# Splitting weight chunks 3 to 13 with two DMAs and a negation instead of a load, a rounding and a subtraction

## The reference

```python
q, k, v = x @ wq.T, x @ wk.T, x @ wv.T          # heads of 128
q, k = rope(q), rope(k)
o = lightning_attention(q, k, v)                # scores * exp(-lam * (i - j)), causal
x = x + o @ wo.T
h = layernorm(x)
x = x + fwht(silu(h @ W1.T) * (h @ W3.T)) @ W2.T
```

## Time and profile before

| | before |
|---|---|
| median of 3 runs | 270.7 us (270.65 to 270.79) |
| profiled execution, its span | 269.5 us |
| PE busy | 261.0 us, 97% |
| DVE busy | 204.9 us, 76% |
| ACT busy | 167.7 us, 62% |
| POOL busy | 143.9 us, 53% |
| granted clock of PE | 1.00 all through |
| read from HBM | 11.93 MB |

### The profile page before, as it was taken

How to read it: one execution, slowest core, us unless ns; L and a number is a source line. 1 busy time by engine, 2 the same in 40 slices (tenths; PEclk the granted TensorE clock), 3 DMA queues, 4 the chain that set the end, 5 groups by cost and what they waited for, 6 DMA issues and landing times.

```text
span 269.5 us, 4222 instructions
## 1 busy us (share of the span) xinstructions
PE 261.0 (97%) x1506; PEld 227.4 (84%) x1506; DVE 204.9 (76%) x336; ACT 167.7 (62%) x283; POOL 143.9 (53%) x105
## 2 busy tenths in 40 slices
PE   7898799999999999999999999999999999999995
PEld 5786488979889888888889889898888879988895
DVE  4799899899979897869899799795575984143333
ACT  3879896875898767556867768984353542043230
POOL 2302989888889467532795897899519200000000
DMA  6594620211220000000020001200000000100002
GB/s 205 189 346 169 243 80 2 78 31 47 80 78 4 0 1 0 4 0 0 2 61 17 2 11 67 80 2 2 0 0 2 0 0 21 59 0 2 0 0 78
DMA packets 5635, 13.23 MB, mean 49 GB/s; under 512 B 624, under 2 KB 2544, under 8 KB 5616
## 3 DMA queue, kind: packets, MB, share of 16 engines
q1 hardware_dynamic: 5040, 12.39, 13.4%
q10 hardware_dynamic: 576, 0.59, 0.6%
HBM read 11.93 MB, written 1.05 MB: 48 GB/s over the span
## 4 chain that ended last, share of the span: by engine, by line
PE 72%; DVE 15%; ACT 5%; issue 4%; DMA 2%; POOL 1%; SPq 0%; DVEq 0%; ACTq 0%
PE bank L317 24%; PE bank L318 24%; PE bank L319 23%; DVE rope_b L1014 2%; DVE rope_a L1013 2%; DMA w_raw<-in_wq 2%; DVE bank L1041 2%; DVE v_hid L1000 1%; PE bank L333 1%; ACT rope_b L661 1%; ACT rope_b L660 1%; DVE qk L1021 1%; DVE rope_b L1065 1%; DVE o_lo L1051 1%; DVE p_lo L1046 1%
## 5 line engine op out<-in xcount | busy, mean ns | idle before, releaser
L843 POOL TENSOR_TENSOR qk<-rope_a,rope_b 128x512 f32<-128x512 f32 x36 | 49.7, 1383 | 25.6 <-DVE rope_b L1014 25.1
L317 PE MATMUL bank<-xt_hi,w_hi 128*128 128x512 f32 x140 | 55.0, 393 | 0.5 <-issue 0.4
L318 PE MATMUL bank<-xt_lo,w_hi 128*128 128x512 f32 x140 | 54.7, 391 | 0.0
L319 PE MATMUL bank<-xt_hi,w_lo 128*128 128x512 f32 x140 | 54.5, 389 | 0.0
L850 POOL TENSOR_TENSOR q_hid<-qk,q_hid 128x512 fp32r<-128x512 f32 x29 | 39.8, 1379 | 10.4 <-ACT q_hid L666 10.4
L673 ACT ACTIVATE p_hi<-bank 128x512 fp32r<-128x512 f32 x48 | 28.6, 596 | 15.7 <-DVE bank L1041 15.2
L1014 DVE TENSOR_TENSOR rope_b<-rope_b,sin_sb 128x512 f32<-128x512 f32 x40 | 37.7, 942 | 0.0
L318 PE MATMUL bank<-w_lo,o_hi 128*128 128x256 f32 x128 | 36.2, 283 | 0.0
L319 PE MATMUL bank<-w_hi,o_lo 128*128 128x256 f32 x128 | 36.2, 283 | 0.0
L317 PE MATMUL bank<-w_hi,o_hi 128*128 128x256 f32 x128 | 36.1, 282 | 0.0
L1013 DVE TENSOR_TENSOR rope_a<-bank,cos_sb 128x512 f32<-128x512 f32 x40 | 27.5, 687 | 10.6 <-ACT rope_b L661 10.1
(11 more groups left out here) (90 smaller groups left out, 614.8 us busy)
## 6 DMA issues: line engine op xcount, KB each, us to landing
w_raw<-in_w SPq DMA_DIRECT2D x6, 512.0 KB, 3.2
decay_sb<-in_decay SPq DMA_DIRECT2D x4, 512.0 KB, 5.3
w_raw<-in_wo SPq DMA_DIRECT2D x4, 512.0 KB, 4.7
w_raw<-in_wq SPq DMA_DIRECT2D x3, 512.0 KB, 3.3
x_sb<-in_x SPq DMA_DIRECT2D x3, 256.0 KB, 7.1
out<-x_sb SPq DMA_DIRECT2D x6, 128.0 KB, 1.8
w_raw<-in_wv SPq DMA_DIRECT2D x1, 512.0 KB, 6.1
w_raw<-in_wk SPq DMA_DIRECT2D x1, 384.0 KB, 6.4
```

The costliest lines, as they stand in the source:

```text
L317: pe.matmul(o, a_hi, b_hi, start=first, stop=False, skip_group_check=shared)
L318: pe.matmul(o, a_hi, b_lo, start=False, stop=False, skip_group_check=shared)
L319: return pe.matmul(o, a_lo, b_hi, start=False, stop=last, skip_group_check=shared)
L843: pool.tensor_tensor(qk[:, r % 2, :], rope_a[:, r % 2, :], rope_b[:, r % 2, :], ALU.add).then_inc(rope_sum_pool, 1)
```

## The change

Chunks 3 to 13 no longer come through `w_raw`. A DMA from POOL reads a chunk from HBM and writes it, converted to fp32r, to `w_hi` (`cast_weights`). ACT writes the negative of that to `w_lo` (`minus_high`, in the places where `high_weights` stood). A second DMA from POOL reads the chunk again and adds it to `w_lo` (`add_weights`), which leaves the chunk minus its high part. `low_weights` is gone for these chunks on POOL and DVE. SP then has only the decay tables, x, the small tables and chunks 0, 1, 2, 14 and 15 to load, and issues the tables earlier.

```diff
-LOW_ON_DVE = (0, 3, 5, 7)
+LOW_ON_DVE = (0,)
+ADDED = range(3, 14)
...
-            if n in LOW_ON_DVE:
+            if n in ADDED:
+                engine.wait_ge(w_added[n], 16)
+            elif n in LOW_ON_DVE:
...
                 if n >= SLOTS:
-                    wait_low_weights(sp, n - SLOTS)
+                    wait_low_weights(sp, n % SLOTS)
...
             load_chunk(2)
+            load_decay(0)
             sp.wait_ge(first_lo, len(FIRST))
-            load_chunk(3)
-            load_decay(0)
-            load_chunk(4)
             load_decay(1)
             load_x(2)
             load_x(3)
-            load_chunk(5)
             load_decay(2)
             load_decay(3)
             sp.dma_start(had_raw[:], hadamard).then_inc(had_loaded, 16)
-            for n in range(6, len(CHUNKS)):
+            for n in range(ADDED.stop, len(CHUNKS)):
                 load_chunk(n)
...
+            def minus_high(n):
+
+                _, _, at = CHUNKS[n]
+                act.wait_ge(w_cast[n], 16)
+                act.activation(w_lo[:, at:at + CH], w_hi[:, at:at + CH].bitcast(F32), ACT.Copy,
+                               scale=-1.0).then_inc(w_minus, 1)
...
             high_v(0, 2)
+            minus_high(3)
             high_rope(("Q", 0, 1))
             high_v(0, 3)
             high_weights(2)
             swap(("Q", 0, 2))
-            high_weights(3)
-            high_weights(4)
+            minus_high(4)
             swap(("Q", 0, 3))
...
                 if unit_chunk(u) is not None:
-                    high_weights(unit_chunk(u))
+                    minus_high(unit_chunk(u))
...
+            def cast_weights(n):
+
+                w, j, at = CHUNKS[n]
+                if n >= CHUNK_NO[("w1", 0)]:
+                    i = (at - AT_Q) // CH
+                    pool.wait_ge(lin_full, LIN_NO[("Q", 1, 4 * i + 3)] + 1)
+                pool.dma_start(w_hi[:, at:at + CH], dram[w][j]).then_inc(w_cast[n], 16)
+
+            def add_weights(n):
+
+                w, j, at = CHUNKS[n]
+                pool.wait_ge(w_minus, n - ADDED.start + 1)
+                pool.dma_start(w_lo[:, at:at + CH], dram[w][j], accum_op=ALU.add).then_inc(w_added[n], 16)
...
-                if unit_chunk(u) is not None and unit_chunk(u) not in LOW_ON_DVE:
-                    low_weights(unit_chunk(u))
+                if unit_chunk(u - 1) is not None and u > FIRST_UNIT:
+                    add_weights(unit_chunk(u - 1))
+                if unit_chunk(u) is not None and u > FIRST_UNIT:
+                    cast_weights(unit_chunk(u))
```

More of the change, by code:

```diff
@@ L195, in build @@
         w_hi_done, had_done = sem("w_hi_done"), sem("had_done")
+        w_minus = sem("w_minus")
+        w_added = {n: sem(f"w_added{n}") for n in ADDED}
+        w_cast = {n: sem(f"w_cast{n}") for n in ADDED}
         w_lo_dve, w_lo_pool = sem("w_lo_dve"), sem("w_lo_pool")
@@ L620, in high_weights @@
                 a = FIRST_OF.get(n, 0)
[L621 to L624 removed]
+                act.wait_ge(w_loaded[n % SLOTS], 16)
                 act.activation(w_hi[:, at + a:at + CH], w_raw[:, n % SLOTS, a:], ACT.Copy).then_inc(w_hi_done, 1)
+            def minus_high(n):
[3 more added lines that the diff above has]
+                               scale=-1.0).then_inc(w_minus, 1)
             def high_x(i, k):
@@ L744, in _ @@
             high_p(0, S_FIRST1)
-            high_weights(5)
-            high_weights(6)
+            minus_high(5)
+            minus_high(6)
             high_rope(("Q", 0, 4))
@@ L753, in _ @@
             high_p(1, S_SECOND)
-            high_weights(7)
+            minus_high(7)
             high_rope(("K", 0, 1))
@@ L767, in _ @@
             high_o(2, 0)
-            high_weights(8)
+            minus_high(8)
             high_rope(("Q", 0, 8))
@@ L864, in butterfly @@
                 else:
-                    pool.wait_ge(w_loaded[n % SLOTS], 16 * (n // SLOTS + 1))
+                    pool.wait_ge(w_loaded[n % SLOTS], 32)
                     if dc:
@@ L882, in _ @@
             low_weights(1)
+            cast_weights(3)
+            cast_weights(4)
+            cast_weights(5)
             low_weights(2)
+            add_weights(3)
+            add_weights(4)
+            cast_weights(6)
             rope_add(("Q", 0, 3))
-            low_weights(4)
             low_rope(("Q", 0, 3))
+            add_weights(5)
             rope_add(("Q", 0, 4))
@@ L890, in _ @@
             rope_add(("K", 0, 1))
+            cast_weights(7)
             low_rope(("Q", 0, 5))
@@ L893, in _ @@
             rope_add(("Q", 0, 6))
-            low_weights(6)
+            add_weights(6)
             rope_add(("Q", 0, 7))
@@ L898, in _ @@
             rope_add(("Q", 0, 8))
+            add_weights(7)
+            cast_weights(8)
             rope_add(("Q", 0, 9))
@@ L906, in _ @@
             rope_add(("Q", 0, 11))
-            low_weights(8)
+            add_weights(8)
+            cast_weights(9)
             for u in range(FIRST_UNIT, UNITS):
@@ L1137, in _ @@
             rotate(("Q", 0, 2))
-            low_weights(3)
             rope_add(("Q", 0, 2))
@@ L1151, in _ @@
             rotate(("Q", 0, 5))
-            low_weights(5)
             mask(1, S_FIRST0)
@@ L1180, in _ @@
             rotate(("K", 0, 2))
-            low_weights(7)
             mask(3, S_SECOND)
```

6 lines of the change are left out of this document (removed).

## The result

The changed kernel takes 316.6 us (median of 4 runs, 315.1 to 320.6) where the kernel before takes 270.7 us: a ratio of 1.167 with an interval of 1.165 to 1.169. Slower was right; 298.0 us was 18.6 us too low, and 316.6 lies outside the range of 284 to 312 us.

A forecast was written before the change was run, and what follows sets the result against it. PE, busy 261.0 of 269.5 us, was taken to bound the kernel. Terms of 9.7 + 2.7 + 2.7 + 12.2 = 27.3 us gave a 296.8 us span, with 1.2 us to the median 298.0 us; range 284 to 312 us.

The forecast's parts named there:

- the last paragraph of the prediction: Signs in the trace: ACT waits 2 to 8 us before negations of chunks 7, 8, 10 to 13, not 5, 6, 9.
- term 1: First addition takes 5.5 us; attend(0,0) on PE starts at 31.9, not 29.81: +2.1 us.
- 2, to scores(2): Add 5 and cast 7 on POOL: scores(2) start at 49.55, not 42.94: +6.6 us, together with term 1.
- term 3: Cast 8 lands at 65.0, ACT's negation ends 5.4 us late; scores(4) at 73.15, not 63.50: +9.7 us by then.
- term 4: Units' loop, chunks 10 and 11: ACT negates after the cast lands; attend(10,0) at 145.2, not 142.52: +2.7 us per chunk.
- Term 5: Loop, chunks 12 and 13, ACT without idle time before either: negation 14.3 us late, up(0,0) on PE delayed: +12.2 us.
- C = 4.0 us: Assumed time from POOL reaching a DMA to its data having landed, in quiet; upper end 6.5 us.
- g = 1.0 us: Assumed time of the POOL instruction that writes a DMA's descriptors; ends 0.4 and 1.5 us.
- PE busy about 261 us as before: Sign in the trace after: PE's busy time unchanged in a longer span, new idle time put down to DVE and POOL.
- Rival B: POOL's DMAs are slower, descriptor writing held or adding at half pace: 306 to 325 us, say 313; 15 in 100.
- The upper end of the unknown costs: The same steps with landing price 6.5 us and POOL's issue at 1.5 us: 317 us.

The follow-up runs named there:

- e7: Changed kernel with SP's loads of chunks 14 and 15 (w2) held back until chunk 3 is added: 312.8 us (ratio 1.157).
- e3: Changed kernel with POOL issuing each converting DMA ahead of the adding DMA beside it (chunks 8, 9, 12, 13): 308.1 us (ratio 1.137).
- e5: Changed kernel with PE multiplying tiles of zeros in seven of its stops, 111 matmuls in all: 311.3 us (ratio 1.150).

## Why the prediction was wrong

The direction, the places and in the main the mechanism were right, and several sizes were not: ACT waits ahead of the negations of chunks 7, 8, 10, 11, 12 and 13 by 2.8 to 9.1 us, and not of 5, 6 and 9, as the last paragraph of the prediction asked. It waited ahead of chunk 3's as well, 1.9 us, which was not forecast. Step by step, what each term added to PE's lag (the fourth column is what the lag gains between stops, matmul by matmul):

| term | forecast, added | measured, added | of it slower matmuls | what differed |
| --- | --- | --- | --- | --- |
| 1, to attend(0,0) | 2.1 | 7.3 | 2.8 | first addition, cast 3, clock |
| 2, to scores(2) | 4.5 | 4.4 | -0.2 | nothing in the sum |
| 3, to scores(4) | 3.1 | 9.3 | 4.9 | cast 8 behind add 7; PE stops at Q11; clock |
| then to 131 us | 0 | 0.8 | 0.8 | |
| 4, chunks 10 and 11 | 5.4 | 6.0 | 0.4 | little in the sum |
| 5, chunks 12 and 13 | 12.2 | 17.9 | 5.7 | casts behind adds; clock |
| sum | 27.3 | 45.75 | 14.4 | |

**What was right.** Terms 2 and 4 rest on a conversion that stands alone on POOL's queue. From POOL's reaching it to its landing it took 3.6 us where I took C = 4.0 us, and each term came out within 0.6 us. For term 4 that is in part luck: the two places that it names gave 2.1 and 2.0 us (166.43 and 191.70) and not 2.7 each, and 1.9 us lie in small stops and slower matmuls between them, which it does not have. The issue, g = 1.0 us, was 0.6 us for a converting and 0.87 us for an adding DMA. Nothing was gained by what is removed, as said.

**The step that failed first: one price C for every DMA.** Term 1 gave the first addition 5.5 us; it landed after 8.3 us, 3 of them for SP's loads of w2, which e7 took away. (Of the 5.2 us that term 1 lacks, 2.8 are this, 1.1 that POOL reached the DMA at 24.54 and not 23.45, and 1.3 the slower matmuls behind.) I had named these loads and priced them at the decay tables' 5.3 us, a row without POOL's DMAs in it. In quiet an adding DMA takes 5.4 us, so the 4.0 us of the text would have been wrong for it too. Terms 3 and 5 gave C = 4.0 us to conversions that stand right behind an adding DMA. They took 6.1 to 6.2 us, and e3 showed that the order does it: the other way round they land 0.5 to 2 us earlier, and 8.4 us of the time come back.

**The second: conversion of chunk 3 at the start.** I let the negation of chunk 3 cost 0.6 us of ACT's time. Its conversion landed 7.7 us after the issue, beside the loads of the start, and ACT waited 1.9 us; PE was 1.4 us late at 22.24 before any term of mine began.

**The third: the clock had no term.** Every step moved PE's work without changing its pace. The rows have some 14 us of slower matmuls behind the stops, of which e5 gets some 5 us back. In term 1, twelve matmuls took 4.15 us (32.97 to 37.12) and not 2.85. "PE busy about 261 us as before" was wrong: it was 276.3.

**The fourth: where term 3 lands.** I followed K2's way to scores(4). PE had stopped before that, for 4.24 us at 78.05, for the rotation that frees the bank of its next product, which hangs on the same ACT queue. At scores(4) itself (84.50) it then had no wait. Term 5 misses the same kind of stop, 6.44 us at 208.45; its two stops add 12.2 us, the forecast's figure, but the forecast had all of it at the second place and with conversions that landed 2 us sooner, so the match is chance.

Three of these were taken away one at a time: the converting DMA behind the adding one (e3, 8.4 us), SP's loads beside the first addition (e7, 3.8 us) and the falls of the clock (e5, 5.3 us). Together that would be 17.5 of the 18.6 us that the forecast lacks, an estimate from their sum; no run has them together.

Rival B, POOL's DMAs slower (306 to 325 us, "say 313"), came nearest to the time and had 15 in 100. That is partly luck, since it has no term for the clock either. Of its two reasons the second was right (adding is slower, 5.4 against 3.6 us). The first, that descriptor writing is held by DVE, is not what the rows show: an issue took 0.6 to 0.9 us, and 1.07 us at most. The long holds found here go the other way, from POOL to DVE. By the Trainium skill, SBUF — State Buffer, section Who interferes with whom, a DVE instruction with two SBUF inputs contends with GpSimd's reads, and the shared port pair is an exclusive lock; for DVE's two-port modes it adds that whoever issues first has the pair for the whole instruction. The 5.27 us agree with the contention, but the block lasted for a row of three of POOL's instructions behind the DMA and not for one.

By the Trainium skill, DMA: Bandwidth & Descriptors, section Anatomy of one DMA, I had put an estimate of 3.2 us beside my 4.0 us; the conversion alone came near it with 3.6 us, the adding DMA with 5.4 us did not.

The upper end of the unknown costs, 6.5 us with g = 1.5, gave 317 us. I had worked that out and left it outside the range; a range that takes in the bounds of the unknown costs would have reached it and held the time.

Open is how large DVE's blocking is in the changed kernel itself. Its trace has one such row (2.60 us at 87.03) and no lag of PE there, so it is small against the waits; no run has taken it away alone.
